# Mixture stage: four hidden tiles made ahead of the chosen experts' term in place of two, and the first split tile of the last product moved ahead of the turned weights

## The chip, the cores and the metric

One core of a Trainium2 chip runs the whole program. The metric is the device time of one execution in microseconds, the median of several runs; lower is better.

## The reference

The program is a small perceiver of six blocks on x (16 x 64 rows of 512) and a context (16 x 512 rows of 512), each block added to x. The change touches the last one only, the mixture of experts:

```
logits = x @ gate_w.T + gate_b;  scores = softmax(logits)
top_v, top_i = top_k(scores, 2);  val_sum = top_v.sum()
for e in range(8):
    gate  = count(top_i == e) * val_sum
    inter = x @ wi.T + bi + (x @ lora_A[e].T) @ lora_B[e].T      # 1024 rows x 2048
    out  += gate * (relu(inter) @ wo.T + bo)
x = x + out
```

All experts share wi and wo; only the term of rank 16 differs. So the kernel makes x @ wi.T once, adds the term of the first chosen expert, takes the relu, adds the difference between the second and the first chosen expert's term to the same sum, takes the relu again, adds the two, and multiplies by wo once.

## The kernel before, in words

Rows stand in 8 groups of 128; the transposed activations xT have 1024 columns, halved into n = 0 and 1. FF = 2048 hidden features are 16 blocks f. A **tile** u = 2f + n is one block f by one half n, 128 x 512, and there are 32. Every product is made of two rounded halves of each operand (high and low), three matmuls per 128 of contraction (`product`, line 256). All engines run lists written out in the code, in order, and meet by semaphores.

TensorE's parts in `tensor` (from line 2492):

- `hidden_pe(f, n, u)`: x @ wi.T of one tile, 12 matmuls of 128x512 (read from xT, wT) into bank (u + 2) % 4. It waits for the split weights of block f (`wt_v`), for tiles 2 and 3 also for the copies of the picked rows out of banks 0 and 1 (`pick_a`), and from tile 4 on for the relu that empties the bank (`relu2` of tile u - 4).
- `pick_chosen_pe(n)`: two matmuls (line 2467) that spread the choice of experts over the partitions, into banks 0 and 1. ScalarE copies them out (line 2707), VectorE multiplies by the down products (2624) and takes a difference (2625), ScalarE and VectorE split the result into the halves of z (264, 273), which signals `z_v`.
- `expert_pe(u)`: 3 matmuls (z, BT) that add the first expert's term; for tiles 0 and 1 it waits for `z_v`. Then ScalarE's relu (line 2719, result h1, two buffers) and `second_pe(u)`, 3 more matmuls after that relu; then VectorE's relu (2638) and sum (2641), which signals `joined`. The relu of tile u waits for `joined` of tile u - 2.
- `turn_weight_pe(w)`: four transposes (line 2420) of a 128-row block of wi (w below 16) or wo (from 16), into bank 6 or 7, then split by ScalarE (`turn_weight_a`) and VectorE (`turn_weight_v`).
- `produce_pe(w)`: the last product. For each of 32 steps (n, f), 12 matmuls (woT, hR) into four sums in banks 4, 5, 2, 3, after ScalarE and VectorE have split the finished tile into hR, and the weight into woT.

Before the loop over tiles the list is: hidden 0, transposes of the choice, turn weight 1, pick(0), hidden 1, pick(1). In the loop a tile u does hidden (from u = 2), expert, every second time a weight, then second of tile u - 1:

```
for u in range(len(tiles) + 1):
    if u < len(tiles):
        if u >= 2:
            hidden_pe(*tiles[u], u)
        expert_pe(*tiles[u], u)
```

In the last product VectorE does, for every w below 16, the split of weight 16 + w and then that of the hR tile; ScalarE likewise.

Of the kernel before, what the change touches and what calls it, by code (L numbers as in the profile page):

```python
# [21 lines left out]
N2 = ROWS // 512  # L22
# [11 lines left out]
FT = FF // P  # L34
# [34 lines left out]
def build(nc, a, out):  # L69
    ctx = ExitStack()  # L70
    pe, dve, act, pool, sp = nc.tensor, nc.vector, nc.scalar, nc.gpsimd, nc.sync
# [10 lines left out]
    with ctx:  # L82
# [177 lines left out]
        def split_a(high, src, scale=None, bias=None):  # L260

            if bias is not None:
                return act.activation(high, src, ACT.Identity, bias=bias)
            return act.copy(high, src) if scale is None else act.mul(high, src, scale)  # L264

        def split_v(low, src, high, scale=None, bias=None):

            rounded = high.bitcast(F32)
            if bias is not None:
                return dve.scalar_tensor_tensor(out=low, in0=src, scalar=bias, in1=rounded, op0=ALU.add, op1=ALU.subtract)  # L270
            if scale is not None:
                return dve.scalar_tensor_tensor(out=low, in0=src, scalar=scale, in1=rounded, op0=ALU.mult, op1=ALU.subtract)
            return dve.tensor_tensor(low, src, rounded, ALU.subtract)  # L273
# [2034 lines left out]
        def l1_mixture():  # L2308
# [58 lines left out]
            joined = signal("f_joined")  # L2367
# [55 lines left out]
            def hidden_pe(f, n, u):  # L2423
                cols = slice(n * 512, (n + 1) * 512)
                pe.wait_ge(wt_v.s, wt_v(2 + f))
                if u >= 4:
                    pe.wait_ge(relu2.s, relu2(u - 4))
                elif u >= 2:
                    pe.wait_ge(pick_a.s, pick_a(u))
                product(bank[:, hb(u), :], lambda h, c: wT[:, f % 2, h, c * P:(c + 1) * P], lambda h, c: xT[:, h, c, cols], C,  # L2430
                        last=False)
# [14 lines left out]
            def produce_pe(w):  # L2446
                n, f = w // FT, w % FT
                pe.wait_ge(hr_v.s, hr_v(w))
                pe.wait_ge(wt_v.s, wt_v(2 + FT + f))
                if w == 0:  # L2450
                    pe.wait_ge(joined.s, joined(N2 * FT - 1))
                for g in range(4):
                    if f == 0 and n:
                        pe.wait_ge(xsum.s, xsum(5 * G + g))
                    ins = product(bank[:, acc[g], :], lambda h, _: hR[:, w % 2, h, g * P:(g + 1) * P],
                                  lambda h, _: woT[:, f, h, :], 1, first=(f == 0), last=(f == FT - 1))
                    if f == FT - 1:
                        ins.then_inc(prod.s, 1)
                if f < FT - 1:
                    ins.then_inc(prod.s, 1)  # L2460

            def pick_chosen_pe(n):
                cols = slice(n * 512, (n + 1) * 512)
                for k in range(2):
                    if n:
                        pe.wait_ge(pick_a.s, pick_a(k))
                    pe.matmul(bank[:, k, :], spread[:, k, :], oneT[:, cols], start=True, stop=True).then_inc(pick_pe.s, 1)  # L2467
# [24 lines left out]
            def tensor():  # L2492
                for c in range(C):
                    ins = pe.transpose(bank[:, 7, c * P:(c + 1) * P], o7[:, c * P:(c + 1) * P], ident[:])
                ins.then_inc(back_pe.s, 1)
                pe.wait_ge(small_in.s, small_in(1))
                for c in range(C):
                    ins = pe.transpose(bank[:, 4, c * P:(c + 1) * P], small[:, 0, c * P:(c + 1) * P], ident[:])
                for c in range(C):
                    ins = pe.transpose(bank[:, 5, c * E:(c + 1) * E], small[0:E, 1, c * P:(c + 1) * P], ident[0:E, 0:E])  # L2500
                ins.then_inc(proj.s, 1)
                for g in range(4):
                    rows_pe(g)
                pe.wait_ge(lb_in.s, lb_in(E - 1))
                lora_b_pe(0)
                lora_b_pe(1)
                rows_pe(4)
                rows_pe(5)
                pe.wait_ge(xt_v.s, xt_v(3))
                pe.wait_ge(wt_v.s, wt_v(1))  # L2510
                logits_pe(0)
                rows_pe(6)
                rows_pe(7)
                lora_b_pe(2)
                lora_b_pe(3)
                pe.wait_ge(xt_v.s, xt_v(G - 1))
                logits_pe(1).then_inc(lg_pe.s, 1)
                pe.wait_ge(bt_v.s, bt_v(3))
                turn_weight_pe(0)
                pe.wait_ge(lg_a.s, lg_a(0))  # L2520
                for g in range(G):
                    ins = pe.transpose(bank[:, 0, g * E:(g + 1) * E], lgT[:, g // 4, (g % 4) * P:(g % 4 + 1) * P],
                                       ident[0:E, 0:E])
                ins.then_inc(lg_pe.s, 1)
                for n in range(N2):
                    cols = slice(n * 512, (n + 1) * 512)
                    product(bank[:, 4 + n, :], lambda h, c: AT[:, h, c, :], lambda h, c: xT[:, h, c, cols], C).then_inc(down.s, 1)
                hidden_pe(*tiles[0], 0)
                pe.wait_ge(one_v.s, one_v(0))
                for g in range(G):  # L2530
                    ins = pe.transpose(bank[0:2 * E, g // 4, (g % 4) * P:(g % 4 + 1) * P],  # L2531
                                       one[:, g, :, :].rearrange("p s e -> p (s e)"), ident[:])
                ins.then_inc(one_pe.s, 1)
                turn_weight_pe(1)
                pe.wait_ge(one_a.s, one_a(0))
                pe.wait_ge(spread_a.s, spread_a(0))
                pick_chosen_pe(0)
                hidden_pe(*tiles[1], 1)
                pick_chosen_pe(1)
                for u in range(len(tiles) + 1):  # L2540
                    if u < len(tiles):
                        if u >= 2:
                            hidden_pe(*tiles[u], u)
                        expert_pe(*tiles[u], u)
                    if u and u % N2 == 0 and u // N2 + 1 < FT:
                        turn_weight_pe(u // N2 + 1)
                    if u:
                        second_pe(*tiles[u - 1], u - 1)
                for w in range(N2 * FT + 1):
                    if w < FT:  # L2550
                        turn_weight_pe(FT + w)
                    if w:
                        produce_pe(w - 1)


            def turn_weight_v(w):
                dve.wait_ge(wt_a.s, wt_a(2 + w))
                at = wT[:, w % 2, :, :] if w < FT else woT[:, w - FT, :, :]
                split_v(at[:, 1, :], bank[:, 6 + w % 2, :], at[:, 0, :]).then_inc(wt_v.s, 1)
# [12 lines left out]
            def vector():  # L2572
# [72 lines left out]
                                                 op0=ALU.mult, op1=ALU.add).then_inc(biased.s, 1)  # L2645
                for w in range(N2 * FT + 1):
                    if w < N2 * FT:
                        if w < FT:
                            turn_weight_v(FT + w)
                        n, f = w // FT, w % FT  # L2650
                        dve.wait_ge(hr_a.s, hr_a(w))
                        split_v(hR[:, w % 2, 1, :], hid(f, n), hR[:, w % 2, 0, :]).then_inc(hr_v.s, 1)
                    if w and (w - 1) % FT == FT - 1:
                        n = (w - 1) // FT
                        for g in range(4):
                            xg = X[:, 4 * n + g, :]
                            dve.wait_ge(prod.s, prod(n * (FT + 3) + FT - 1 + g))
                            dve.wait_ge(biased.s, biased(G - 1))
                            dve.scalar_tensor_tensor(out=xg, in0=bank[:, acc[g], :], scalar=m1[:, 4 * n + g:4 * n + g + 1],  # L2659
                                                     in1=xg, op0=ALU.mult, op1=ALU.add).then_inc(xsum.s, 1)  # L2660
# [18 lines left out]
            def scalar():  # L2679
# [41 lines left out]
                        turn_weight_a(u // N2 + 1)  # L2721
                for w in range(N2 * FT):
                    n, f = w // FT, w % FT
                    if w < FT:
                        turn_weight_a(FT + w)
                    act.wait_ge(joined.s, joined(f * N2 + n))
                    if w >= 2:
                        act.wait_ge(prod.s, produced(w - 2))
                    split_a(hR[:, w % 2, 0, :], hid(f, n)).then_inc(hr_a.s, 1)

            def store():
                for g in range(G):
# [56 lines left out]
```

## Time and profile before

| | us |
|---|---|
| median of 3 runs | 1337.64 (1336.24 to 1343.86) |
| the profiled execution | 1346.65 |
| its span, first to last instruction | 1345.4 |
| TensorE busy in it | 1254.3 (93%) |
| mean granted TensorE clock | 0.964 |

The profiled execution is 1.25 us longer than its span, and 9.0 us longer than the median of the runs that were only timed. The mixture stage takes the last 280 us or so of the span; its loop over tiles begins at about 1098 us, the last product at about 1245 us.

### The profile page before, as it was taken

Reading aid. Unit: us, or ns where it says so; the run is one execution under the profiler, and the core shown is the slowest. Engines: PE = TensorE matmul, PEld = TensorE weight load, DVE = VectorE, ACT = ScalarE, POOL = GpSimd, SP = SyncE. Lnnn points to the kernel's source line nnn. Section 1 sums busy time; section 2 is a strip of 40 time slices with the busy share of each in tenths; the row PEclk is TensorE's granted clock in tenths of the full one; section 3 lists DMA queues with packets and bytes.
Section 4 is the critical chain, followed back from the end, with each engine's and each line's share of the span. In section 5 each row is a group of like instructions: output and inputs, shape, how many; then the busy total and the mean of one; then the engine's idle time right before and its main releaser. Section 6 shows DMA issues by size and latency. Waiting matters only on the chain. (4 is left out here: it accounts for less than half of the span.)

```text
span 1345.4 us, 25936 instructions
## 1 busy us (share of the span) xinstructions
PE 1254.3 (93%) x11101; PEld 934.8 (69%) x11101; DVE 732.0 (54%) x1572; ACT 518.1 (39%) x1018; POOL 137.3 (10%) x158
## 2 busy tenths in 40 slices
PE   6999889989677999999999999999898879999999
PEld 4554478856334777777777777776787758887787
DVE  4358486535597455555545555555584745434332
ACT  2234437422113255445454545445353332222221
POOL 2200021234331300000000000000031100000000
PEclk9899989879978999999999999999899989999999
DMA  9659600000121411111000100110400100010100
GB/s 278 256 178 404 232 0 1 0 1 1 31 102 47 158 63 34 40 54 36 33 33 33 34 33 33 35 53 11 80 1 1 69 3 32 32 32 32 63 32 32
DMA packets 49334, 88.23 MB, mean 66 GB/s; under 512 B 19210, under 2 KB 20284, under 8 KB 45124
## 3 DMA queue, kind: packets, MB, share of 16 engines
q1 hardware_dynamic: 48160, 86.01, 18.7%
q8 instruction: 88, 1.44, 0.4%
q10 hardware_dynamic: 1060, 0.56, 0.2%
q14 instruction: 26, 0.21, 0.0%
HBM read 65.59 MB, written 20.97 MB: 64 GB/s over the span
## 5 line engine op out<-in xcount | busy, mean ns | idle before, releaser
L1856 ACT ACTIVATE K<-bank,vecT 128x512 f32<-128x512 f32 x64 | 44.1, 689 | 171.4 <-PE bank L256 171.4
L1871 ACT ACTIVATE W<-W,low 128x512 f32<-128x512 f32 x128 | 91.0, 713 | 47.3 <-DVE low L1775 47.3
L186 POOL TENSOR_TENSOR rstd<-rstd,half_pow 128x1 f32<-128x1 f32 x48 | 29.8, 628 | 721.0 <-DVE rstd L182 721.0
L1775 DVE CUSTOM_DVE_ANT_0 W<-bank,W 128x512 f32<-128x512 f32 x128 | 80.8, 688 | 40.5 <-PE bank L1644 40.5
L1753 DVE TENSOR_TENSOR W<-bank,vecT 128x256 f32<-128x256 f32 x16 | 6.8, 425 | 167.5 <-PE bank L1665 167.5
L256 PE MATMUL bank<-woT,hR 128*128 128x512 f32 x384 | 94.8, 403 | 2.2 <-DVE hR L273 2.2
L256 PE MATMUL bank<-xT,wT 128*128 128x512 f32 x384 | 95.3, 397 | 0.0
L256 PE MATMUL bank<-Wkv,Wq 128*128 128x512 f32 x384 | 93.9, 400 | 0.0
L256 PE MATMUL bank<-Wq,Wkv 128*128 128x512 f32 x384 | 93.0, 394 | 0.0
L256 PE MATMUL bank<-ctxT,Wkv 128*128 128x512 f32 x384 | 92.5, 394 | 0.5 <-DVE ctxT L273 0.5
L256 PE MATMUL bank<-Wkv,ctxT 128*128 128x512 f32 x384 | 92.9, 394 | 0.0
L256 PEld LDWEIGHTS bank<-Wkv,Wq 128*128 128x128 f32 x384 | 71.7, 190 | 27.5 <-issue 13.0
L256 PEld LDWEIGHTS bank<-Wkv,ctxT 128*128 128x128 f32 x384 | 70.8, 188 | 27.2 <-issue 12.2
L256 PEld LDWEIGHTS bank<-woT,hR 128*128 128x128 f32 x384 | 72.0, 191 | 18.9 <-DVE hR L273 2.5
L256 PEld LDWEIGHTS bank<-xT,wT 128*128 128x128 f32 x384 | 72.6, 189 | 17.9 <-issue 0.4
L256 PEld LDWEIGHTS bank<-ctxT,Wkv 128*128 128x128 f32 x384 | 70.9, 188 | 15.6 <-issue 0.9
L256 PEld LDWEIGHTS bank<-Wq,Wkv 128*128 128x128 f32 x384 | 70.8, 188 | 14.8
L1878 ACT COPY PT<-bank 128x512 f32<-128x512 f32 x128 | 65.8, 600 | 21.6 <-PE bank L206 21.6
L1783 DVE TENSOR_SCALAR W<-W,total 128x512 f32<-128x512 f32 x128 | 62.3, 487 | 4.6
L2719 ACT ACTIVATE h<-bank,vecT 128x512 f32<-128x512 f32 x32 | 22.0, 689 | 107.6 <-PE bank L256 107.6
L206 PEld LDWEIGHTS bank<-ident,W 32*128 32x128 f32 x2752 | 47.0, 139 | 21.0 <-issue 12.2
L256 PE MATMUL bank<-z,BT 128*128 128x512 f32 x192 | 55.0, 410 | 5.9 <-DVE z L273 5.8
(350 smaller groups left out, 2264.4 us busy)
## 6 DMA issues: line engine op xcount, KB each, us to landing
W<-ctx_turned SPq DMA_DIRECT2D x16, 1024.0 KB, 4.8
W<-in_ctx_dram SPq DMA_DIRECT2D x8, 1024.0 KB, 10.8
ctx_turned<-ctxT SPq DMA_DIRECT2D x8, 1024.0 KB, 7.6
ctx_turned<-W SPq DMA_DIRECT2D x8, 1024.0 KB, 6.9
XT<-in_ctx_dram SPq DMA_DIRECT2D x4, 1024.0 KB, 12.0
XT<-in_L_ffn_wi_dram SPq DMA_DIRECT2D x4, 1024.0 KB, 6.1
XT<-in_L_ffn_wo_dram SPq DMA_DIRECT2D x4, 1024.0 KB, 5.1
raw_own<-in_ctx_dram SPq DMA_DIRECT2D x3, 1024.0 KB, 11.2
```

Of the source, the lines that this page charges most:

```text
L186: pool.tensor_tensor(rstd[:, g:g + 1], rstd[:, g:g + 1], half_pow[:], ALU.pow).then_inc(rstd_ok.s, 1)
L206: ins = pe.transpose(bank[:, first + r, to:to + 32], src_of(t, k)[strip, :], ident[strip, strip])
L256: ins = pe.matmul(dst, stationary(x, k), moving(y, k), start=(first and n == 0), stop=(last and n == len(passes) - 1), skip_group_check=True)
L1753: dve.tensor_tensor(oT[:, (i // 2) % 2, :, (i % 2) * NP:(i % 2 + 1) * NP], src.rearrange("f (c n) -> f c n", c=C), bias, ALU.add).then_inc ...
L1775: dve.tensor_tensor_reduce(out=PR[:, j, :], in0=bank[:, 4 + j % 4, :], in1=mask, scale=1.0, scalar=3.0e38, op0=ALU.add, op1=ALU.min, accum ...
L1783: dve.tensor_scalar(PR[:, j, :], PR[:, j, :], total[:, j:j + 1], None, ALU.mult).then_inc(probs.s, 1)
L1856: act.activation(K[:, m, :], bank[:, n % 4, :], ACT.Identity, bias=pcol("L1_xattn_bk", m)).then_inc(ring_a.s, 1)
L1871: act.activation(PR[:, j, :], PR[:, j, :], ACT.Exp, bias=low[:, j:j + 1], scale=-1.0, accum_out=total[:, j:j + 1]).then_inc(expd.s, 1)
L1878: act.copy(PT[:, 4 * half:4 * half + 4, :, strip].rearrange("p t k n -> p (t k) n"), bank[:, 4 + n % 4, :].rearrange("p (a n) -> p a n", n ...
L2719: act.activation(h1[:, u % 2, :], bank[:, hb(u), :], ACT.Relu, bias=pcol("L1_ffn_bi", f)).then_inc(relu1.s, 1)
```

## The change

TensorE makes the hidden products of tiles 2 and 3 right behind pick(1), ahead of the first `expert_pe`. At the start of the last product, ScalarE and VectorE split the first tile into hR before they split weight 16, not after it, and TensorE's wait for the last joined tile is moved from the start of the product to its third group.

```diff
             def produce_pe(w):
                 pe.wait_ge(hr_v.s, hr_v(w))
                 pe.wait_ge(wt_v.s, wt_v(2 + FT + f))
-                if w == 0:
-                    pe.wait_ge(joined.s, joined(N2 * FT - 1))
                 for g in range(4):
+                    if w == 0 and g == 2:
+                        pe.wait_ge(joined.s, joined(N2 * FT - 1))
...
                 hidden_pe(*tiles[1], 1)
                 pick_chosen_pe(1)
+                for u in (2, 3):
+                    hidden_pe(*tiles[u], u)
                 for u in range(len(tiles) + 1):
                     if u < len(tiles):
-                        if u >= 2:
+                        if u >= 4:
                             hidden_pe(*tiles[u], u)
...
# VectorE, last product (ScalarE the same with turn_weight_a and split_a)
-                        if w < FT:
+                        if 0 < w < FT:
                             turn_weight_v(FT + w)
                         n, f = w // FT, w % FT
                         dve.wait_ge(hr_a.s, hr_a(w))
                         split_v(hR[:, w % 2, 1, :], hid(f, n), hR[:, w % 2, 0, :]).then_inc(hr_v.s, 1)
+                        if w == 0:
+                            turn_weight_v(FT)
```

TensorE's list from pick(1) on, before (z, BT are expert and second; xT, wT are hidden; ident, XT turns a weight):

```order
L2467 MATMUL bank<-oneT,spread 128x512 [waits f_pick_a] x2
L256 MATMUL bank<-z,BT 128x512 [waits f_z_v]
L256 MATMUL bank<-z,BT 128x512 x2
L256 MATMUL bank<-z,BT 128x512 [waits f_z_v]
L256 MATMUL bank<-z,BT 128x512 x2
L256 MATMUL bank<-z,BT 128x512 [waits f_relu1]
L256 MATMUL bank<-z,BT 128x512 x2
L256 MATMUL bank<-xT,wT 128x512 [waits f_pick_a,wt_v]
L256 MATMUL bank<-xT,wT 128x512 x11
```

And in the changed kernel:

```order
L2467 MATMUL bank<-oneT,spread 128x512 [waits f_pick_a] x2
L256 MATMUL bank<-xT,wT 128x512 [waits f_pick_a,wt_v]
L256 MATMUL bank<-xT,wT 128x512 x11
L256 MATMUL bank<-xT,wT 128x512 [waits f_pick_a,wt_v]
L256 MATMUL bank<-xT,wT 128x512 x11
L256 MATMUL bank<-z,BT 128x512 [waits f_z_v]
L256 MATMUL bank<-z,BT 128x512 x2
L256 MATMUL bank<-z,BT 128x512 [waits f_z_v]
L256 MATMUL bank<-z,BT 128x512 x2
L256 MATMUL bank<-z,BT 128x512 [waits f_relu1]
L256 MATMUL bank<-z,BT 128x512 x5
L2420 MATMUL bank<-ident,XT 128x128 [waits half_in_0,wt_v]
```

24 matmuls that wait for no z now stand ahead of the two groups that do; behind these, expert and second groups of four tiles follow each other without a hidden product between them.

VectorE's list at the end of the tiles, before (the last two rows of the loop, then the last product):

```order
L2638 TENSOR_SCALAR W_late<-bank,vecT 128x512 [waits f_sec_pe]
L2641 TENSOR_TENSOR W_late<-W_late,h 128x512 [waits f_relu2]
L273 TENSOR_TENSOR woT<-bank,woT 128x512 [waits wt_a]
L273 TENSOR_TENSOR hR<-W,hR 128x512 [waits f_hr_a]
L273 TENSOR_TENSOR woT<-bank,woT 128x512 [waits wt_a]
```

And in the changed kernel:

```order
L2640 TENSOR_SCALAR W_late<-bank,vecT 128x512 [waits f_sec_pe]
L2643 TENSOR_TENSOR W_late<-W_late,h 128x512 [waits f_relu2]
L273 TENSOR_TENSOR hR<-W,hR 128x512 [waits f_hr_a]
L273 TENSOR_TENSOR woT<-bank,woT 128x512 [waits wt_a] x2
```

The first split of hR and the first of woT have changed places; both still stand behind the last tile's sum.

## Rows read from the trace of the kernel before

**Rows 1.** The page: the span, and each engine's busy time
```profile
span 1345.4 us, 25936 instructions
PE 1254.3 (93%) x11101; PEld 934.8 (69%) x11101; DVE 732.0 (54%) x1572; ACT 518.1 (39%) x1018; POOL 137.3 (10%) x158
```
**Rows 2.** Timeline, TensorE, 1095 to 1118: start us, us, instruction [idle before <-releaser]
```profile
1095.00 3.07 PE L256 MATMUL bank<-xT,wT 128*128 128x512 f32 x12
1098.00 0.73 PE L2467 MATMUL bank<-oneT,spread 16*128 16x512 f32 x2
1101.50 0.96 PE L256 MATMUL bank<-z,BT 128*128 128x512 f32 x3 [2.77 <-DVE z L273]
1105.52 2.93 PE L256 MATMUL bank<-z,BT 128*128 128x512 f32 x6 [3.06 <-DVE z L273]
1108.25 3.52 PE L256 MATMUL bank<-xT,wT 128*128 128x512 f32 x12
...
1117.62 2.96 PE L256 MATMUL bank<-xT,wT 128*128 128x512 f32 x12
```
**Rows 3.** Timeline, ScalarE and VectorE, 1094 to 1106
```profile
1094.80 0.69 DVE L273 TENSOR_TENSOR wT<-bank,wT 128x512 fp32r<-128x512 f32 x1 [5.58 <-ACT wT L264]
1095.57 1.41 DVE L2624 TENSOR_TENSOR W<-W,bank 128x512 f32<-128x512 f32 x2
1098.53 1.07 ACT L2707 COPY W<-bank 128x512 f32<-128x512 f32 x2 [2.58 <-PE bank L2467]
1100.15 1.29 DVE L273 TENSOR_TENSOR z<-W,z 128x512 fp32r<-128x512 f32 x2 [2.45 <-ACT z L264]
1101.36 1.40 DVE L2624 TENSOR_TENSOR W<-W,bank 128x512 f32<-128x512 f32 x2
1104.17 1.29 DVE L273 TENSOR_TENSOR z<-W,z 128x512 fp32r<-128x512 f32 x2 [0.68 <-ACT z L264]
```
**Rows 4.** Timeline, a steady stretch of the loop over tiles, 1117 to 1122
```profile
1117.82 0.75 DVE L2638 TENSOR_SCALAR W<-bank,vecT 128x512 f32<-128x512 f32 x1 [1.38 <-PE bank L256]
1120.42 0.86 PE L256 MATMUL bank<-z,BT 128*128 128x512 f32 x3
1121.32 0.69 ACT L2719 ACTIVATE h<-bank,vecT 128x512 f32<-128x512 f32 x1 [3.50 <-PE bank L256]
1121.91 0.58 ACT L264 CAST wT<-bank 128x512 fp32r<-128x512 f32 x1
1122.26 2.96 PE L256 MATMUL bank<-xT,wT 128*128 128x512 f32 x12
```
**Rows 5.** The chain that ended last, the same stretch: start us, us, what
```profile
1121.28 0.44 PE bank L2420 x4
1121.72 8.38 PE bank L256 x36
```
**Rows 6.** Busy time by stretch: the first row all engines, then TensorE's busy time, clock, DMA
```profile
1090.00:1101.50 11.50, 8.07 (x39) 5.52 (x37) 4.11 (x7) 4.67 (x8) 0.00 (x0) 1.00 0.00 0
1101.40:1104.00 2.60, 0.96 (x3) 0.74 0.00 0
1246.00:1247.00 1.00, 1.00 (x4) 0.50 0.00 0
```
**Rows 7.** Timeline, the start of the last product, 1241 to 1250
```profile
1241.72 1.03 PE L2420 MATMUL bank<-ident,XT 128*128 128x128 f32 x8
1242.83 0.62 ACT L264 CAST hR<-W 128x512 fp32r<-128x512 f32 x1
1243.04 0.69 DVE L2641 TENSOR_TENSOR W_late<-W_late,h 128x512 f32<-128x512 f32 x1
1243.65 0.68 DVE L273 TENSOR_TENSOR woT<-bank,woT 128x512 fp32r<-128x512 f32 x1
1244.25 0.68 DVE L273 TENSOR_TENSOR hR<-W,hR 128x512 fp32r<-128x512 f32 x1
1244.99 4.62 PE L256 MATMUL bank<-woT,hR 128*128 128x512 f32 x12 [2.24 <-DVE hR L273]
```

More of the change, by code:

```diff
@@ L2723, in scalar @@
                     n, f = w // FT, w % FT
-                    if w < FT:
+                    if 0 < w < FT:
                         turn_weight_a(FT + w)
@@ L2729, in scalar @@
                     split_a(hR[:, w % 2, 0, :], hid(f, n)).then_inc(hr_a.s, 1)
+                    if w == 0:
+                        turn_weight_a(FT)
             def store():
```

## The prediction

> **What bounds the kernel now.** I read the page first: TensorE is busy 93% of the span and no other engine over 54% [rows 1], so time is won only where TensorE waits or runs at the lower clock. Then the timeline at the two places that the diff touches, the chain of waits for the steady pace between them, and the table by stretch for the clock. The reader is to see two waits of TensorE for the halves of z, 2.77 and 3.06 us with three matmuls between them [rows 2], and one of 2.24 us at the start of the last product [rows 7]. Around these the chain is TensorE alone: 36 matmuls in 8.38 us, 0.233 us each, and 0.44 us for four transposes [rows 5]. So what TensorE gains before tile 4 comes out at the end in full, as long as ScalarE and VectorE keep up.
>
> **The first part of the change.** Nothing is added or removed, no DMA moves and SyncE's and GpSimd's lists stay; 24 matmuls of tiles 2 and 3 go from behind the two waits to ahead of them. I count from the end of pick(1) to the start of hidden 4, in the profile's time.
>
> Before: pick(1) starts at 1098.00, two matmuls, so its place ends at 1098.47; hidden 4 starts at 1117.62 [rows 2]. That is 19.15 us. The work between is hidden 2 and 3 (24 matmuls), expert 0 to 3 (12), second 0 to 2 (9) and one turned weight: 45 x 0.233 + 0.44 = 10.9 us. The other 8.2 us are the gap to 1101.50 (3.0), the gap from 1102.20 to 1105.52 (3.3), and 1.9 us of lower clock: the mean granted clock is already 0.74 in the stretch that holds the first three matmuls, that is part at 2.4 and part at 1.2 GHz [rows 6], and the six from 1105.52 take 2.73 us to the next start, 0.455 each [rows 2].
>
> After, step by step:
>
> - Hidden 2 waits for weight 1, split at 1095.5, and for the copy out of bank 0. The two copies start at 1098.53 and take 1.07 together [rows 3], so bank 0 is free at 1099.1; bank 1 is free long before hidden 3 wants it. A wait of 0.65 us is left. Hidden 2 and 3 run 1099.1 to 1104.7 (24 x 0.233 = 5.6).
> - Expert 0 needs the z that came at 1101.44: it runs at once, to 1105.4. Expert 1 needs the second z, ready at 1105.46 [rows 3], so it starts at 1105.52 as before, a wait of 0.1, and ends at 1106.2. The z chain itself (copy, multiply, difference, split) starts from pick(1), which hasn't moved.
> - ScalarE's relu starts 0.43 us after the last of the three matmuls has started, and takes 0.69 [rows 4], where the last of the three from 1120.42 starts at 1120.89 and the relu at 1121.32. So relu 0 is done at 1106.3, second 0 runs 1106.4 to 1107.1, a wait of 0.15.
> - Expert 2 to 1107.8, weight 2 turned to 1108.2, second 1 to 1108.9, expert 3 to 1109.6.
> - Here the new wait comes in. Relu 2 needs `joined` of tile 0: VectorE's relu starts 0.43 after second 0's last start, at 1107.3, takes 0.75 [rows 4], and the sum takes 0.69 [rows 7], to 1108.8. Relu 2 then runs to 1109.5; second 2 starts at 1109.6, just in time, and ends at 1110.3.
> - ScalarE's split of weight 2 is queued behind relu 2: from 1109.4 for 0.58 [rows 4], VectorE's half 0.69 more [rows 3], so hidden 4 can start at 1110.75. A wait of 0.45 us is left.
>
> The sum: 10.9 us of work and 1.35 us of waits from 1098.47, so hidden 4 starts at 1110.75 in place of 1117.62: **6.9 us earlier**, 5.0 of waits and 1.9 of clock. Behind it nothing gives it back: VectorE has two relus, two sums, two additions to X (costed like a relu) and one weight split per pair of tiles, about 5.1 us of the pair's 8.8, so its delay of about a tile is gone by hidden 6, and the weights' loads are needed only from block 4 on.
>
> The clock is a term that I can only bound. In the stretch 1090 to 1101.5 it stayed at 1.00 although TensorE was busy only 8.07 of 11.5 us [rows 6], so waits of 0.1 to 0.65 us shouldn't lower it, and I take none. For what the two long waits cost, the bounds are nothing (the clock may fall at another moment in another execution) and about twice the 1.9 seen; I take the row. The gain is then 5.0 to 8.8. The Trainium skill, TensorE: Matmul & The Clock Gate, Part 1, says that the gate's timing isn't reset when a kernel starts, so that the number of slow matmuls differs from run to run; by that the 1.9 is one draw of several, which no row of one execution can show.
>
> **The second part of the change** I cost at nothing. The first matmul of the last product needs hR, woT and the `joined` of the last tile. ScalarE's halves aren't last: hR is done at 1243.45, while VectorE is at the last sum until 1243.73 [rows 7]. VectorE then does two splits of 0.68, woT and hR, and TensorE starts at 1244.99, right behind the second. The change swaps the two; both still stand behind the sum in VectorE's list, and TensorE still needs both. The moved wait for `joined` is met before either. The bounds: nothing, and one split's step, 0.6 us, if one of them could leave the path. Against that gain is the order of VectorE's list, so I take nothing. What TensorE loses there stays: 2.24 us of wait and 4.62 us for 12 matmuls, which elsewhere take 2.8.
>
> **Sum.** Against the profiled execution: 1346.65 - 6.9 = 1339.8. Against the median of the runs: 1337.64 - 6.9 = **1330.7**, 0.52% less. A measurement of this kernel can tell about 0.5%, 6.7 us, from no change, so the forecast sits right at the bound of 1330.95.
>
> **The rivals.**
>
> - *Waits go, the clock's part doesn't show.* In timed runs the two long waits lowered the clock less than in the profiled one, or the small new waits lower it. For: one execution is all I have. Against: the two waits are long and close together. The gain is 5.0: 1332.6.
> - *The last product keeps its clock.* All of it starts 6.9 us earlier, and the 2.24 us wait may fall otherwise to the clock's change at 1246 [rows 6]. The gain is up to 4.62 - 2.80 = 1.8 more: 1328.9.
> - *The backlog is worse than counted.* Four tiles' relus stand back to back. If relu 2 and relu 3 each wait a whole round of second, VectorE's relu and sum, and ScalarE's relu (0.43 + 0.75 + 0.69 + 0.69 = 2.6 us) where I have 0.45 once, or if VectorE's z work slows down because TensorE now writes PSUM beside it, 2 to 4 us come back: about 1334. Against the second: the pair of multiplies took 1.41 us beside hidden 1 and 1.40 with TensorE idle [rows 3].
> - *The swap at the last product works after all:* 0.6 more, 1330.1.
> - *Slower: the moved tiles run at the lower clock.* If the short waits bring the clock down at about 1099 and keep it there, each of the 45 matmuls costs 0.455 in place of 0.233. It decides from 31 matmuls on (6.9 / 0.222); all 45 cost 10.0, which is 3.1 us slower than before: 1340.7. Against it is the clock of 1.00 through similar waits [rows 6]. The Trainium skill, the same page, section on psum-queue depth-cycling, reports such a case: short idle times between groups of matmuls, as banks are cycled, made the clock swing. By it the time would be that of this rival; in 1090 to 1101.5 the trace disagrees.
>
> **How the numbers follow.** Forecast as worked out 0.50, at the bound, so 0.26 beyond it and 0.24 within; clock's part missing 0.20, within 0.5%; last product keeps its clock 0.11, faster; backlog 0.08, within; the swap works 0.06, faster; lower clock 0.05, of which 0.03 is slower by over 0.5% (if it lasts into further tiles, or the run scatters). Together: faster 0.43, within 0.54, slower 0.03. The range: from 1328 (the last product's clock, and some scatter) to 1336 (the backlog case, and the scatter that the runs of before show upward from 1336.24). It leaves out the slower case and about as much below.
>
> **What would show it.** Right: no long wait of TensorE ahead of expert 0 and expert 1; 24 matmuls of xT, wT in 5.6 us right behind pick(1); a wait of about 0.65 us ahead of them and about 0.45 ahead of hidden 4, with "DVE wT" as its releaser; clock 1.00 from 1099 to 1112; hidden 4 at about 1110.75 in the profile's time (some 12.3 us after pick(1) ends); and the last product still behind a wait of 2.24 us, with VectorE's woT as its releaser now. Wrong: clock below 1.00 in that stretch, hidden 4 later than 14 us after pick(1), waits of TensorE for ScalarE's relu in tiles 4 to 7, or a wait ahead of the last product that is shorter by over 0.3 us.

## The result and the profile after

Over 20 runs of each kernel the changed one takes 1333.74 us (1323.51 to 1339.71), the one before 1342.16 (1329.67 to 1346.49). The ratio is **0.9944, 95% interval 0.9919 to 0.9968**: faster by 0.3 to 0.8%, that is 4.3 to 10.9 us. The forecast was 6.9 us, 0.52%. The absolute time is 3.0 us above the forecast 1330.7, which was made from a median of three runs of before that lies 4.5 us under that of all 20; it is inside the range of 1328 to 1336.

The profile page of the changed kernel:

```profile
span 1333.3 us, 25936 instructions
PE 1246.2 (93%) x11101; PEld 929.9 (70%) x11101; DVE 731.5 (55%) x1572; ACT 517.9 (39%) x1018; POOL 137.1 (10%) x158
```

Against [rows 1] the span is 12.1 us shorter. Not all of that is the change. pick(1), up to which TensorE's list is the same in both, starts at 1092.22 in place of 1098.00: 5.8 us were won ahead of the change, by luck (see the last section). From the start of pick(1) to the end of the span it is 1333.3 - 1092.22 = 241.1 us in place of 247.4: **6.3 us for the change**. This stretch is what I compare from here on, because it scatters far less from one execution to the next: where two kernels have the same code in it, their profiles agree within 0.1 us, but for one fall of the clock at the last product (see the last section). Each kernel has one profile.

TensorE's timeline of the changed kernel from pick(1) to tile 4 (answers to [rows 2, 4]):

```profile
1092.22 0.73 PE L2467 MATMUL bank<-oneT,spread 16*128 16x512 f32 x2
1093.48 5.84 PE L256 MATMUL bank<-xT,wT 128*128 128x512 f32 x24 [0.53 <-ACT W L2711]
1099.15 3.30 PE L256 MATMUL bank<-z,BT 128*128 128x512 f32 x12
1102.29 0.60 PE L2420 MATMUL bank<-ident,XT 128*128 128x128 f32 x4
1102.64 2.50 PE L256 MATMUL bank<-z,BT 128*128 128x512 f32 x9
1105.38 3.06 PE L256 MATMUL bank<-xT,wT 128*128 128x512 f32 x12 [0.24 <-DVE wT L273]
```

Both long waits are gone. The 24 moved matmuls stand right behind pick(1), and what is left is 0.53 us for ScalarE's copy and 0.24 us for VectorE's split of weight 2, with two waits inside the groups that the merged rows hide. (The profile counts a wait from the modelled end of the matmul before it. The prediction gives each matmul 0.233 us of place; by that count the first wait is 1.26 - 0.47 = 0.79 us.) ScalarE and VectorE beside it (answers to [rows 3, 4]):

```profile
1092.75 1.07 ACT L2711 COPY W<-bank 128x512 f32<-128x512 f32 x2 [2.58 <-PE bank L2467]
1098.40 1.30 DVE L273 TENSOR_TENSOR z<-W,z 128x512 fp32r<-128x512 f32 x2 [0.69 <-ACT z L264]
1100.06 1.38 ACT L2723 ACTIVATE h<-bank,vecT 128x512 f32<-128x512 f32 x2 [1.17 <-PE bank L256]
1101.87 0.75 DVE L2640 TENSOR_SCALAR W<-bank,vecT 128x512 f32<-128x512 f32 x1 [1.89 <-PE bank L256]
1103.44 0.69 ACT L2723 ACTIVATE h<-bank,vecT 128x512 f32<-128x512 f32 x1 [2.00 <-DVE W L2643]
1104.02 0.58 ACT L264 CAST wT<-bank 128x512 fp32r<-128x512 f32 x1
1104.63 0.69 DVE L273 TENSOR_TENSOR wT<-bank,wT 128x512 fp32r<-128x512 f32 x1 [1.29 <-ACT wT L264]
```

The second z split starts 6.18 us after pick(1), as before (6.17): the moved matmuls don't slow it down. The last four rows are the new chain that was forecast: VectorE's relu of tile 0, its sum, relu 2 on ScalarE, the split of weight 2 queued behind it, then hidden 4.

TensorE's busy time by stretch (answers to [rows 6]). The columns are the stretch, its length, TensorE's busy time with the number of matmuls, the granted clock (1.00 is the 2.4 GHz level, 0.50 the 1.2), the DMA share and GB/s:

```profile
1088.00:1094.00 6.00, 4.91 (x18) 1.00 0.00 0
1094.00:1099.00 5.00, 5.00 (x23) 1.00 0.02 3
1099.00:1105.40 6.40, 6.08 (x28) 1.00 0.00 0
1105.40:1120.00 14.60, 14.60 (x67) 1.00 0.20 72
1233.40:1236.80 3.40, 3.40 (x10) 0.50 0.00 0
```

The clock stays at the 2.4 GHz level through the whole start of the loop; at the last product it still falls to 1.2. There (answers to [rows 7]):

```profile
1229.57 1.04 PE L2420 MATMUL bank<-ident,XT 128*128 128x128 f32 x8
1230.89 0.69 DVE L2643 TENSOR_TENSOR W_late<-W_late,h 128x512 f32<-128x512 f32 x1
1231.51 0.68 DVE L273 TENSOR_TENSOR hR<-W,hR 128x512 fp32r<-128x512 f32 x1
1232.11 1.28 DVE L273 TENSOR_TENSOR woT<-bank,woT 128x512 fp32r<-128x512 f32 x2
1232.94 4.58 PE L256 MATMUL bank<-woT,hR 128*128 128x512 f32 x12 [2.33 <-DVE woT L273]
```

The splits have changed places, and TensorE waits as long as it did: 2.33 us in place of 2.24.

### The profile page after: what moved, and what is told of

It is laid out like the page before. It is cut to its first block and busy times, and to the rows that moved or that the text cites. A ratio compares the mean times of both kernels' runs of the same rounds, so it can differ in the third digit from the quotient of the medians.

```text
span 1333.3 us, 25936 instructions
## 1 busy us (share of the span) xinstructions
PE 1246.2 (93%) x11101; PEld 929.9 (70%) x11101; DVE 731.5 (55%) x1572; ACT 517.9 (39%) x1018; POOL 137.1 (10%) x158
## 5 line engine op out<-in xcount | busy, mean ns | idle before, releaser
L206 PEld LDWEIGHTS bank<-ident,W 32*128 32x128 f32 x2752 | 47.4, 140 | 20.9 <-issue 12.1
L206 PE MATMUL bank<-ident,W 32*128 32x32 f32 x2752 | 52.1, 226 | 3.5 <-DVE W L1783 2.6
## 6 DMA issues: line engine op xcount, KB each, us to landing
W<-in_ctx_dram SPq DMA_DIRECT2D x8, 1024.0 KB, 10.4
```

Of the source, the lines that this page charges most:

```text
L206: ins = pe.transpose(bank[:, first + r, to:to + 32], src_of(t, k)[strip, :], ident[strip, strip])
```

## The experiments

All times of the table are us from the one profile of each kernel; "end" is the end of its span. A timed ratio further down is to runs of the kernel before made beside it: their median was 1336.66 us beside the first four experiments and 1340.79 beside the other four, so absolute times of the two groups don't compare.

| kernel | pick(1) to hidden 4 | pick(1) to last product | last product to end | pick(1) to end |
|---|---|---|---|---|
| before | 19.62 | 146.99 | 100.41 | 247.40 |
| changed | 13.16 | 140.72 | 100.36 | 241.08 |
| tiles only | 13.19 | 140.67 | 100.38 | 241.05 |
| swap only | 19.64 | 147.12 | 100.35 | 247.47 |
| one tile | 16.62 | 144.08 | 100.38 | 244.46 |
| filled waits | 17.84 | 145.21 | 98.87 | 244.08 |
| weight 2 split first | 12.79 | 140.24 | 100.37 | 240.61 |
| splits ahead | 13.19 | 139.48 | 98.78 | 238.26 |
| turned ahead | 13.19 | 138.76 | 98.78 | 237.54 |
| both places | 12.79 | 138.26 | 98.78 | 237.04 |

**Theory:** the first part of the change is the whole gain, by 5 us of waits and 1.9 us of clock; the second part does nothing because of its place in VectorE's list. **Rivals:** the swap carries some of it; each tile moved is worth the same, and the clock plays no part; the last wait ahead of hidden 4 is VectorE's backlog.

### Tiles only

The kernel before with this alone:

```diff
+                for u in (2, 3):
+                    hidden_pe(*tiles[u], u)
                 for u in range(len(tiles) + 1):
                     if u < len(tiles):
-                        if u >= 2:
+                        if u >= 4:
                             hidden_pe(*tiles[u], u)
```

> Only the first part of the change: hidden 2 and 3 ahead of expert 0; the last product as before. If this part is the whole gain (my theory), TensorE goes from the start of pick(1) to the start of hidden 4 in 13.2 us as in the changed kernel (before: 19.6), the last product starts behind a wait of about 2.24 us for VectorE's split of hR, and the time is about 6.5 us (0.5%) under before. Rival, the swap at the last product carries part of it: the timed gain is clearly smaller than the changed kernel's, and the stretch from hidden 4 to the last product is longer than the changed kernel's 127.6 us by 0.5 us or more.

Measured: 13.19 us to hidden 4, 127.48 us from there to the last product, its wait 2.23 us, 241.05 us to the end, against 241.08 with both parts. So this part is the whole gain. Timed in 12 runs, the ratio to before is 0.9972 (0.9943 to 1.0002), which by itself separates it neither from no change nor from the changed kernel's 0.9944: the scatter of whole executions is larger than the effect, and the verdict rests on the stretch.

### Swap only

```diff
-                        if w < FT:
+                        if 0 < w < FT:
                             turn_weight_v(FT + w)
                         n, f = w // FT, w % FT
                         dve.wait_ge(hr_a.s, hr_a(w))
                         split_v(hR[:, w % 2, 1, :], hid(f, n), hR[:, w % 2, 0, :]).then_inc(hr_v.s, 1)
+                        if w == 0:
+                            turn_weight_v(FT)
```

with the same on ScalarE and the later wait for `joined`.

> Only the second part: hR of the first tile split before weight 16, and the later wait for joined; tiles as before. My theory: nothing, because VectorE makes both splits behind the last tile's sum and TensorE needs both; the wait ahead of the last product is 2.2 to 2.35 us, now for woT; the ratio to before is 1.00 within its interval. Rival, one split leaves the path: that wait is about 1.6 us and the time 0.6 us lower, or up to 2.4 us if the clock then stays up.

Measured: 247.47 us to the end (before 247.40), the wait 2.32 us, ratio 1.0014 (0.9981 to 1.0047). Nothing, as expected. The wait is 0.09 us longer wherever the swap is in (2.32 or 2.33 in four kernels) than where it isn't (2.23 or 2.24 in three); I did not look for the reason.

### One tile

The changed kernel with `for u in (2,)` ahead of the loop, and `if u >= 3` in it.

> Tile 2 alone ahead of expert 0, tile 3 back in the loop. By my count the wait for the first z goes and a wait of about 2.7 us for the second z stays. If waits alone cost time, hidden 4 starts 15.0 us after the start of pick(1) (before 19.6, both tiles 13.2): 4.6 of the 6.5 us are won. If the remaining wait still lowers the clock, as the 2.24 us wait at the last product does, about 1.7 to 1.9 us of that are lost again and it is 16.7 to 16.9. Rival, each tile is worth the same: 16.4, with the clock at 1.00.

```profile
1085.64 0.73 PE L2467 MATMUL bank<-oneT,spread 16*128 16x512 f32 x2
1086.90 3.05 PE L256 MATMUL bank<-xT,wT 128*128 128x512 f32 x12 [0.53 <-ACT W L2711]
1089.79 0.86 PE L256 MATMUL bank<-z,BT 128*128 128x512 f32 x3
1093.17 3.76 PE L256 MATMUL bank<-z,BT 128*128 128x512 f32 x9 [2.52 <-DVE z L273]
1102.26 2.96 PE L256 MATMUL bank<-xT,wT 128*128 128x512 f32 x12
```

TensorE by stretch, its clock the number behind the count:

```profile
1089.00:1093.00 4.00, 1.66 (x8) 1.00 0.00 0
1093.00:1097.00 4.00, 3.83 (x11) 0.59 0.01 4
```

Hidden 4 comes 16.62 us after pick(1). With one wait of 2.52 us left (2.7 was expected) the clock falls behind it, and the nine matmuls take 3.6 us to the next start, where nine at the full clock take 2.1. The time alone hardly parts the two cases: 16.6 lies between the 16.7 of the low clock and the 16.4 of equal shares. The clock does: 0.59 is the forecast mechanism, and the rival wanted 1.00. So 3.0 us come from the first tile and 3.5 from the second. Without the low clock the expectation put hidden 4 at 15.0, and the second tile would have been worth only about 1.8; it is worth more because it takes the last long wait away and the low clock with it. The timed ratio is 0.9969 (0.9936 to 1.0002), and can't show it.

### Filled waits

The kernel before, with dummy matmuls in the two waits; nobody reads their sums. A wait for the split of weight 1, which they read, is added ahead of the loop.

```diff
                 if u < N2:
+                    product(bank[:, 7, :], lambda h, c: wT[:, 1, h, c * P:(c + 1) * P], lambda h, c: xT[:, h, c, 0:512], C)
                     pe.wait_ge(z_v.s, z_v(2 * n + 1))
...
                 pick_chosen_pe(1)
+                pe.wait_ge(wt_v.s, wt_v(3))
```

> The kernel before, with 12 matmuls of 128x512 in each of the two waits for z, into bank 7; nobody reads their sums. The waits stay, TensorE isn't idle in them. If the lower clock behind the waits is a cost of its own (1.9 us by my count), hidden 4 starts 17.7 us after the start of pick(1) in place of 19.6, with the clock at 1.00 in between, and the time is some 1.9 us lower although 24 matmuls are added. Rival, the waits are the whole cost: 19.6 or later. If the added matmuls delay the z chain by sharing PSUM, the z splits of VectorE come later than 5.94 us (start of the second) after pick(1)'s start plus 0.2.

```profile
1088.12 0.73 PE L2468 MATMUL bank<-oneT,spread 16*128 16x512 f32 x2
1088.78 3.06 PE L256 MATMUL bank<-xT,wT 128*128 128x512 f32 x12
1091.68 0.90 PE L256 MATMUL bank<-z,BT 128*128 128x512 f32 x3
1092.42 2.96 PE L256 MATMUL bank<-xT,wT 128*128 128x512 f32 x12
1095.65 1.65 PE L256 MATMUL bank<-z,BT 128*128 128x512 f32 x6 [0.27 <-DVE z L273]
1105.96 2.96 PE L256 MATMUL bank<-xT,wT 128*128 128x512 f32 x12
```

```profile
1094.30 1.30 DVE L273 TENSOR_TENSOR z<-W,z 128x512 fp32r<-128x512 f32 x2 [0.69 <-ACT z L264]
```

```profile
1088.00:1106.00 18.00, 17.73 (x77) 1.00 0.00 1
```

Expert 1 starts 7.53 us after pick(1), as before (7.52), yet hidden 4 comes at 17.84 in place of 19.62. That is the clock by itself: **1.8 us**, bought with work that does nothing. Over the 18 us the granted clock is 1.00. (In the kernel before it was at 0.50 from about 1102.6 to 1109.5; TensorE worked in the last 3.9 us of that, at half the pace, and about half of 3.9 is what came back.) The second z split starts 6.18 us after pick(1) here. By the sign of the expectation, 5.94 plus 0.2, that would be a delay; but the 5.94 is wrong, [rows 3] give 6.17 for the kernel before, and so there is none. Of the changed kernel's 6.46 us the clock is thus 1.8 and the waits 4.7. The timed ratio, 1.0009 (0.9976 to 1.0043), can't show it: both no change and 1.8 us less lie inside its interval.

This kernel showed one thing more, at its last product, where nothing was changed:

```profile
1233.33 3.07 PE L256 MATMUL bank<-woT,hR 128*128 128x512 f32 x12 [2.24 <-DVE hR L273]
```

The same wait of 2.24 us as before, and this time the clock did not fall: 3.07 us for 12 matmuls in place of 4.62 [rows 7], and 98.87 us to the end in place of 100.41.

### Weight 2 split first

On ScalarE, in the changed kernel:

```diff
                 for u in range(len(tiles) + 1):
+                    if u == 2:
+                        turn_weight_a(2)
...
-                    if u and u % N2 == 0 and u // N2 + 1 < FT:
+                    if u > 2 and u % N2 == 0 and u // N2 + 1 < FT:
                         turn_weight_a(u // N2 + 1)
```

> The changed kernel, but ScalarE splits weight 2 before the relu of tile 2, not behind it. If the 0.24 us that TensorE waits ahead of hidden 4, and the wait inside the group before, come from that order on ScalarE (relu 2 waits for joined of tile 0, the split stands behind it), hidden 4 starts 12.7 to 12.8 us after the start of pick(1), 0.4 earlier than the 13.2 of the changed kernel, and TensorE's wait there goes. Rival, VectorE's backlog sets it: it stays at 13.1 to 13.2.

```profile
1081.89 0.73 PE L2467 MATMUL bank<-oneT,spread 16*128 16x512 f32 x2
1092.62 0.59 ACT L264 CAST wT<-bank 128x512 fp32r<-128x512 f32 x1 [1.49 <-PE bank L2420]
1093.13 0.69 ACT L2725 ACTIVATE h<-bank,vecT 128x512 f32<-128x512 f32 x1
1093.24 0.69 DVE L273 TENSOR_TENSOR wT<-bank,wT 128x512 fp32r<-128x512 f32 x1 [0.20 <-ACT wT L264]
1094.68 2.96 PE L256 MATMUL bank<-xT,wT 128*128 128x512 f32 x12
```

Hidden 4 comes at 12.79 us, with no wait ahead of it, 0.37 us earlier, and it is 240.61 to the end, 0.47 less. Only one execution was timed beside this, so it rests on the profile alone. The order on ScalarE was the cause of the last wait, not VectorE's backlog.

### Splits ahead

In the changed kernel VectorE makes both first splits ahead of the last tile's relu and sum, and the third group of the product waits for tile 29, which empties its banks:

```diff
+                    if u == len(tiles):
+                        dve.wait_ge(hr_a.s, hr_a(0))
+                        split_v(hR[:, 0, 1, :], hid(0, 0), hR[:, 0, 0, :]).then_inc(hr_v.s, 1)
+                        turn_weight_v(FT)
                     if u:
                         f, n = tiles[u - 1]
                         dve.wait_ge(sec_pe.s, sec_pe(u - 1))
...
-                        pe.wait_ge(joined.s, joined(N2 * FT - 1))
+                        pe.wait_ge(joined.s, joined(N2 * FT - 3))
```

> The changed kernel, but VectorE makes the first split of hR and that of weight 16 before the relu and sum of the last tile, not behind them; TensorE's third group waits for the tile whose bank it takes. My theory of why the swap did nothing is that both splits stand behind the last sum. Then the last product starts 1.3 us earlier (126.2 to 126.3 us after hidden 4 in place of 127.6), behind a wait of 1.0 in place of 2.33 us. With so short a wait I expect the clock to stay at 1.00 and the first 12 matmuls to take 3.05 us in place of 4.6, another 1.5 to 1.8. Rival, the path then goes through something else (relu 31, weight 17): the product starts earlier but waits inside its second step.

```profile
1230.07 0.68 DVE L273 TENSOR_TENSOR hR<-W,hR 128x512 fp32r<-128x512 f32 x1
1230.79 0.69 DVE L273 TENSOR_TENSOR woT<-bank,woT 128x512 fp32r<-128x512 f32 x1
1231.39 0.74 DVE L2644 TENSOR_SCALAR W_late<-bank,vecT 128x512 f32<-128x512 f32 x1
1231.62 3.05 PE L256 MATMUL bank<-woT,hR 128*128 128x512 f32 x12 [1.06 <-DVE woT L273]
1234.86 3.04 PE L256 MATMUL bank<-woT,hR 128*128 128x512 f32 x12
```

The product starts 1.2 us earlier behind a wait of 1.06 us, at the full clock, and its second step follows at the usual pace, so the rival, a wait inside the second step, is out. 238.26 us to the end: 2.8 less than the changed kernel. Timed, the ratio to before is 0.9913 (0.9884 to 0.9943). Of the 2.8 us, 1.2 are the wait and 1.6 the clock. This is what an edit at this place can win and the swap can't.

### Turned ahead

Beside that, TensorE turns weights 16 and 17 ahead of second 31, ScalarE splits the first hR ahead of relu 31, and VectorE one tile earlier (TensorE's part):

```diff
+                    if u == len(tiles):
+                        turn_weight_pe(FT)
+                        turn_weight_pe(FT + 1)
                     if u:
                         second_pe(*tiles[u - 1], u - 1)
```

> As the run before, and weights 16 and 17 are turned ahead of second 31, and ScalarE and VectorE split the first hR one tile earlier. The last product starts 2.1 us earlier than in the changed kernel (125.4 to 125.6 us after hidden 4), behind a wait of 0.7 to 0.8 us, at the full clock: 3.6 to 3.9 us in all. If the clock falls there whatever the wait, only 2.1.

```profile
1223.00 1.03 PE L2420 MATMUL bank<-ident,XT 128*128 128x128 f32 x8
1223.79 0.94 PE L256 MATMUL bank<-z,BT 128*128 128x512 f32 x3
1225.42 3.04 PE L256 MATMUL bank<-woT,hR 128*128 128x512 f32 x12 [0.70 <-DVE woT L273]
```

125.57 us from hidden 4 to the last product, a wait of 0.70 us, the clock up: 237.54 us to the end, 3.5 less than the changed kernel, just under the 3.6 to 3.9 that were expected. The ratio to before is 0.9919 (0.9889 to 0.9949).

### Both places

The last two edits that helped, together: weight 2 split first, and the turned-ahead version of the last product.

> The two runs before put together (weight 2 split first, and the last product's operands ahead). If the pieces add up, from the start of pick(1) to the end of the span it is 4.3 us less than the 241.1 of the changed kernel: 236.8, and 10.6 us less than the 247.4 of the kernel before, 0.8% of the time. If the early split of weight 2 only moves the wait, 0.4 less than that.

Measured: 237.04 us from pick(1) to the end, 10.4 less than before and 4.0 less than the changed kernel. The measured pieces, 0.47 and 3.54, add up to that; the expectation, 236.8, was 0.2 too low. Timed in 12 runs: 1328.56 us, ratio 0.9933 (0.9903 to 0.9963). It beats both kernels in the stretch; the timed ratios of the last three versions, 0.991 to 0.993, overlap, so which of them is best rests on the profiles.

## Why the prediction was right

By its own steps:

- **What bounds the kernel.** Right. What TensorE won ahead of tile 4 came out at the end: 6.46 us at hidden 4, 6.32 at the end of the span. Of the 0.14 lost in between 0.10 is hidden 4 itself: behind its wait it takes 2.90 us to the next start, in place of 2.80 in the kernel before and with weight 2 split first, where it follows without a wait. The swap's longer wait, 0.09, is mostly won back behind it, 100.36 us to the end in place of 100.41.
- **The first part, 6.9 us.** The mechanism was right in each step, the size 0.4 too large. Counted from the start of pick(1), hidden 2 was put at 1.1 us and came at 1.26, relu 0 at 7.6 and came at 7.84, VectorE's relu 0 at 9.3 and came at 9.65, relu 2 at 10.8 and came at 11.22, hidden 4 at 12.75 and came at 13.16. The 24 matmuls took 5.67 us, not 5.6. The rest is handovers: up to relu 2 each step of the chain lost about 0.1 us more than the steady rows gave, and I had rounded some of them away.
- **The new wait.** Named rightly, with its cause: relu 2 waits for the sum of tile 0, and the split of weight 2 stands behind it. The run with the split first took it away.
- **The clock, 1.9 of the 6.9.** Right, and shown by itself: 1.8 us with filled waits. The kernel before and the swap alone show the same fall (19.62 and 19.64 us to hidden 4). Two profiles don't show what the clock costs in every execution, since at the last product its fall behind one and the same wait differed, and the bounds "nothing to twice" stay for the timed runs.
- **The second part, nothing.** Right, and for the reason given. The run with both splits ahead of the last sum shows what an edit at this place can win: 1.2 us of wait and 1.6 of clock. I had bounded it at 0.6 us, one split's step, because I looked only at the order that the change makes. The 4.62 us "for 12 matmuls, which elsewhere take 2.8" were misread: 2.8 is the time to the next start, and what compares with 4.62 is the 3.07 of the filled waits, so a clock kept at the last product is worth 1.5 us and not the 1.8 of the rival.

The absolute time owes something to luck: the gain in the timed runs came out above the stretch's 6.3 us and the median of three below that of 20, and the range, which had been stretched upward for scatter, took in both.

Of the rivals, the waits without the clock's part (a gain of 5.0) are contradicted by the profiles but lie inside the timed interval of 4.3 to 10.9 us. The low clock over the moved tiles did not come: 1.00 through waits of 0.53 and 0.24 us. The Trainium skill, TensorE: Matmul & The Clock Gate, section on psum-queue depth-cycling, reports a clock that swings under short idle times between groups of matmuls; no trace here shows that, behind waits of up to 1.06 us. The rival that the last product keeps its clock did not happen in the changed kernel's profile but did in that of the filled waits, one of seven with such a wait, so it is a real draw of 1.5 us. The chance of 0.54 for "within 0.5%" against 0.43 for faster came from a forecast right at that bound; the measured 0.56% lies just beyond it, and its interval holds both.

## What to carry to other kernels

When an engine waits for a chain of short steps, look for work on its own list that needs none of them and whose banks and operands are free already; what is won is the wait and also what the lower clock behind it costs, so the last long wait removed can be worth more than the first (3.5 us against 3.0 here). Swapping two steps changes nothing as long as both stand behind the step that sets the time and the reader needs both: find the last thing ahead of both, and move them past that. And compare kernels over the stretch that the change touches when whole executions scatter more than the effect.

## What the runs showed of the hardware

**Ahead of the change the same list scatters by 16 us, and it is TensorE's pace, not its waits.** Up to pick(1), all ten profiled kernels have the same list, and pick(1) started anywhere from 1081.89 to 1098.36 us, while the stretch behind it repeated within 0.1 us where the same code ran, but for the clock's draw at the last product (below). Two rows of the table by stretch, the first 200 us of TensorE in the kernel before and in the changed one:

```profile
0.00:200.00 200.00, 180.22 (x1720) 0.95 0.64 227
```
```profile
0.00:200.00 200.00, 178.85 (x1747) 0.98 0.64 227
```

The mean clock over the whole span was 0.964 and 0.972 in these two, 0.967 in the kernel with the latest pick(1) and 0.979 in the one with the earliest. Up to pick(1) TensorE was busy 1002.2 us in the earliest and 1018.5 in the latest, with the same matmuls, and idle 79.7 and 79.9; over all ten the idle time was 79.7 to 81.6. The rows up to pick(1), earliest and latest:

```profile
0.00:1081.89 1081.89, 1002.21 (x10043) 0.98 0.22 74
```
```profile
0.00:1098.36 1098.36, 1018.45 (x10043) 0.96 0.21 73
```

So nearly all of the scatter is in how long the same matmuls took. That the clock is the cause of all of it is argued from these numbers: no run changed the clock there by itself.

**The same wait costs the clock in one execution and not in the next.** Ahead of the last product, waits of 2.23 to 2.33 us stood in seven profiles. In six the clock fell within about a microsecond of TensorE's restart and the 12 matmuls took 4.58 to 4.62 us; in one it didn't, and they took 3.07. Behind waits of 1.06 and 0.70 us (three profiles) it never fell. What a fall costs here is 1.5 us each time. The Trainium skill, TensorE: Matmul & The Clock Gate, Part 1, says that the gate runs freely and isn't reset by the kernel. That fits these rows; none of them shows what set the two cases apart. The Trainium skill, the same page, names in its table of goals (Why this matters for your kernels) idle gaps between bursts of matmuls as what makes the throughput drop. These traces show such a drop behind gaps of 2.23 to 2.33 us, in six of seven.
